# Moving the fixed places of layer norm, transpose and node products of the next four graphs in the first pass of a two-layer graph kernel

## The reference: what is computed

```python
D = jnp.abs(x[:, :, None, :] - x[:, None, :, :])
h = jnp.einsum('bijc,oc->bijo', D, W1) + b1
m = jnp.mean(h, axis=(0, 1, 2))
v = jnp.mean((h - m) ** 2, axis=(0, 1, 2))
h = (h - m) / jnp.sqrt(v + EPS) * g1 + be1
h = _leaky(h)
s = jnp.einsum('bijo,uo->biju', h, W2)[..., 0] + b2[0]
s = jnp.where(A_init > 0, s, NEG)
A = jax.nn.softmax(s, axis=-1)
```

## Time and profile before

| what | value |
|---|---|
| median of three runs | 1147.15 us (1144.66 to 1148.58) |
| the profiled execution: time | 1145.85 us |
| its span in the trace | 1143.7 us |
| PE busy | 1055.3 us, 92% of the span |
| DVE busy | 1037.4 us, 91% |
| ACT busy | 1002.7 us, 88% |
| POOL busy | 558.6 us, 49% |

### The profile page before, as it was taken

One profiled execution on the slowest core, in us unless ns is written; L12 is line 12 of the kernel. 1 busy time (PEld: TensorE's weight loads), 2 busy tenths in 40 slices (PEclk: granted clock), 3 DMA queues, 4 the chain that ended last, 5 costly groups with the idle time before them and its releaser, 6 DMA issues.

```text
span 1143.7 us, 17677 instructions
## 1 busy us (share of the span) xinstructions
PE 1055.3 (92%) x6486; PEld 473.0 (41%) x6486; DVE 1037.4 (91%) x1382; ACT 1002.7 (88%) x1268; POOL 558.6 (49%) x314
## 2 busy tenths in 40 slices
PE   3999999999999999999999989999999999965997
PEld 1333333333333433333333444233333333355997
DVE  5999999999999999999999975999999999845887
ACT  4888999999999999999999969999999999814987
POOL 6586668777767867767777700111122213101420
PEclk9999999999999999999999989999999999987999
DMA  6443444444444444444444497999999999650012
GB/s 180 165 158 156 166 168 173 176 157 183 177 169 185 170 175 157 184 179 173 164 166 194 179 354 247 354 350 318 351 331 335 344 328 347 238 155 1 29 48 74
DMA packets 99059, 233.30 MB, mean 204 GB/s; under 512 B 9120, under 2 KB 46464, under 8 KB 98976
## 3 DMA queue, kind: packets, MB, share of 16 engines
q1 hardware_dynamic: 86704, 219.97, 52.4%
q0 software_dynamic: 2240, 7.34, 1.7%
q10 hardware_dynamic: 10032, 4.89, 1.6%
HBM read 124.43 MB, written 107.74 MB: 203 GB/s over the span
## 4 chain that ended last, share of the span: by engine, by line
PE 50%; DVE 27%; ACT 15%; issue 7%; ACTq 1%; POOL 0%; DMA 0%; DVEq 0%
PE psum L767 17%; DVE store L294 11%; PE psum L777 9%; ACT store L654 7%; PE psum L781 7%; DVE plain_st L1075 5%; PE psum L877 4%; ACT store L573 3%; PE psum L757 1%; PE psum L985 1%; DVE store L1107 1%; PE psum L967 1%; PE psum L950 1%; PE psum L968 1%; DVE ln_st L1012 1%
## 5 line engine op out<-in xcount | busy, mean ns | idle before, releaser
L294 POOL TENSOR_TENSOR store<-h_ext 128x2048 f32<-128x2048 f32 (+1 forms) x96 | 386.7, 4030 | 119.8 <-PE psum L767 115.9
L767 PE MATMUL psum<-store,w1tt_sb 128*64 128x512 f32 x1792 | 421.4, 598 | 19.4 <-ACT store L573 19.1
L294 DVE TENSOR_TENSOR store<-psum,h_ext 128x2048 f32<-128x2048 f32 x160 | 363.7, 2273 | 1.3 <-ACT h_ext L543 1.3
L573 ACT ACTIVATE store<-store 128x2048 f32<-128x2048 f32 x160 | 305.0, 1929 | 11.3 <-DVE store L294 8.1
L654 ACT ACTIVATE store<-store,st 128x1024 f32<-128x1024 f32 x192 | 227.9, 1240 | 0.0
L767 PEld LDWEIGHTS psum<-store,w1tt_sb 128*64 128x64 f32 x1792 | 122.2, 136 | 254.6 <-issue 224.8
L777 PE MATMUL psum<-store,w_twice 128*64 128x512 f32 x768 | 201.1, 601 | 7.0 <-DVE early L1040 3.5
L294 DVE TENSOR_TENSOR store<-h_ext 128x2048 f32<-128x2048 f32 x64 | 146.3, 2286 | 17.2 <-PE psum L767 17.2
L1075 DVE BATCH_NORM_STATS2 plain_st<-store 128x6 f32<-128x512 f32 x256 | 160.4, 676 | 0.0
L781 PE MATMUL psum<-early 128*64 128x512 bf16 x1152 | 158.2, 380 | 0.0
L877 PE MATMUL psum<-store,w_rows 128*32 128x512 f32 x1024 | 135.2, 610 | 8.9 <-ACT store L654 8.9
(11 more groups left out here) (163 smaller groups left out, 1129.3 us busy)
## 6 DMA issues: line engine op xcount, KB each, us to landing
kept_products<-store SPq DMA_DIRECT2D x192, 512.0 KB, 2.7
store<-kept_products SPq DMA_DIRECT2D x192, 512.0 KB, 5.5
early<-score_skew POOLq DMA_DIRECT2D x14, 384.0 KB, 6.7
early<-adj SPq DMA_DIRECT2D x16, 256.0 KB, 3.6
early<-adj_t SPq DMA_DIRECT2D x16, 256.0 KB, 3.6
store<-x ACTq DMA_DIRECT2D x16, 256.0 KB, 5.3
out<-early SPq DMA_DIRECT2D x16, 256.0 KB, 2.3
score_skew<-early POOLq DMA_DIRECT2D x14, 128.0 KB, 6.0
```

Of the source, the lines that this page charges most:

```text
L294: return engine.tensor_tensor(t[:, :, 0:steps, :], nodes.unsqueeze(2).broadcast_to([C, 2, steps, N]), windows(h_ext[:, 2 * c, :], STEP * m ...
L573: nc.scalar.activation(t, t, ACT.Abs).then_inc(abs_ready, 1)
L767: last = nc.tensor.matmul(t[MID * g:MID * g + MID, b, :], w1tt_sb[:, 0:MID], diff[slot][:, g, b * BANK:b * BANK + BANK], start=True, stop= ...
```

## The change

One line of numbers:

```diff
-NORM_AT, TURN_AT, EXT_AT, NODE_AT, HIGH_AT, REST_AT, MID_AT, PLACE_AT, LOW_AT = 3, 4, 5, 6, 7, 10, 10, 12, 16
+NORM_AT, TURN_AT, EXT_AT, NODE_AT, HIGH_AT, REST_AT, MID_AT, PLACE_AT, LOW_AT = 2, 3, 5, 6, 8, 11, 11, 12, 16
```

## The result

The changed kernel takes 1166.69 us (median of four runs, 1166.54 to 1166.96) beside 1146.59 us for the kernel before, a ratio of 1.0175 with a 95% interval of 1.0157 to 1.0194. It is 20 us slower, where about 7 us less were forecast. The forecast of the likeliest case was wrong; the time is that of the rival which got a chance of 0.06, the lock between `low` and POOL's difference (whichever of the two starts second stands until the first is over), priced at 1168 us "at worst".

The account below looks back on a forecast made before the run. PE was taken to bound clean stretches and DVE the full ones. Terms −6.2 (clean quads), −0.9 (ends of DVE-bound stretches) and 0 (start) gave −7.1 us, so 1140.0 us beside 1147.15; own range 1137 to 1143, wider range 1136 to 1147.

Parts of the forecast that it names:

- What bounds the kernel: First pass: PE, DVE and ACT nearly full; PE sets the pace in clean stretches, DVE is full in others.
- the two kinds of stretch: Clean stretches, where shortening PE's waits pays, and stretches where statistics or bias fill DVE and the saving vanishes.
- Places 2 and 3: normalise and turn moved sooner: PE's hole before chunk 5 shrinks, 0.78 us per clean quad, −6.2 us over eight.
- clean quad: A quad in a stretch where PE sets the pace; eight were counted, each with one PE hole of 0.98 us.
- The 0.2 us of hole that I left standing: PE's wait before chunk 5, forecast to remain at about 0.2 us in place of 0.98.
- The late start of chunk 2: On PE, chunk 2 starts 0.07 us late for its absolute value, absorbed by the 0.2 us hole.
- Places 8, 11 and 11: high, rest and middle moved later: ACT's wait in high goes, rest delays DVE by 0.34 us; costed at nothing.
- the rival on the slower side: low slips behind POOL's place 17 difference and is blocked, 3.8 us longer; 1153 to 1168 us, chance 0.06.
- PE runs that much sooner: At 113.50 normalise, 1.54 us, fills ACT's idle time; DVE uses only 0.43 us; the start summed to 0.
- The price: Blocked low: 3.8 us longer, DVE slack hides 1.2; 2.6 us a quad in eight quads, 1168 us at worst.

Follow-up runs that it names:

- The other half: Only high, rest and middle a chunk later (8, 11 and 11), normalise and turn left at 3 and 4, against the kernel before: 1144.94 us, ratio 0.9983.

## Why the prediction was wrong, point by point

- **What bounds the kernel**: right, and the two kinds of stretch were the right distinction. The same distinction was then not applied to the lock.
- **Places 2 and 3.** The mechanism was right, and so was its size. The whole change brings 1.01 us a clean quad where the lock is kept away (39.29 to 38.28 us). The other half brings 0.19 of it by itself (39.29 to 39.10), which leaves 0.82 for this one; 0.78 was forecast. The 0.2 us of hole that I left standing is not listed as a wait, but the pair of chunks 4 and 5 takes 3.78 us in place of 3.60. The late start of chunk 2, forecast at 0.07 us, is some 0.2 (a pair of 3.81 against 3.60 us).
- **Places 8, 11 and 11.** Put at nothing; by themselves they brought 2.3 us, 0.2%. The lead of `low` fell to 0.26 us; "0.4 us are left" overstated it.
- **The step that failed** is the margin in the rival on the slower side: "The change pushes `low` 0.34 later and POOL, which hangs on PE, not: 0.4 us are left". POOL does move. After a late chunk 2 the chain over PE to POOL's difference is 1.7 us shorter (29.28 in place of 30.98 us), and DVE's own, 29.7 us, cannot follow. The 0.77 us was read in clean quads, where DVE waits 1.86 us for PE at the count of chunk 7 and can come sooner by that much when PE does. In quad 3 the lead was 0.77 as well, but the wait that kept it was 0.43: together 1.2 us of room against 1.7. I had the parts: "PE runs that much sooner, of which DVE can use only its 0.43 us wait" stands in the prediction, as a gain in time that is lost, and was not carried over to POOL, which hangs on PE. The first block came there, at 143 us.
- **The second half of the failure** is the view of quads as independent. I asked what one block costs; with the new places a block makes the next. That the entry could be at one place and the price be paid in every later clean quad was not considered, so the chance of 0.06 was far too small.
- **The price.** One block is as priced, 3.65 us longer. That the sum of 1168 us lies near the measured 1166.69 is in part luck. I took 2.6 us for each of eight clean quads and added them to the time of before. Against the unblocked quad of the new places a blocked one costs 2.29 us (40.57 against 38.28), but against the quad of before only 1.28 (39.29). On the other side 11 quads were blocked and not eight, and where DVE has no slack a block costs the whole: from `low` 3 to `low` 4 it was 45.40 us in place of 41.74, and from 8 to 9 45.39 in place of 41.73.
- **The lock.** The Trainium skill, SBUF — State Buffer, section "Who interferes with whom", says that the second to issue is blocked for the whole of the other's instruction. The rows agree: the 4.06 us end 0.28 us behind POOL's 4.20 us that began 0.42 us before, and so do the 3.65 us where POOL began 0.84 us before.

## What to carry to other kernels

Before moving work that makes one engine run ahead, list the pairs of instructions on two other engines that exclude each other, and read their distance in every kind of stretch, the full ones above all, from the last point that both depend on. A margin that a wait maintains is gone when the wait is gone. And where a loop can be in two modes, a small local change is priced by the mode it leaves the loop in, not by its own length: look for one long instruction that repeats once a period.

## What the runs showed of the hardware that I had not expected

- A DVE subtraction of 256 columns with two SBUF operands took 4.06 us in place of 0.40 when POOL's 2048-column subtraction had begun 0.42 us before it; begun 0.26 us after `low`'s own start, POOL's took 4.23 us and `low` 0.41, so neither lost anything measurable. With one of its operands in PSUM the same subtraction took 0.41 us when POOL's had begun 0.41 us before it, and 0.41 us wholly inside one of POOL's.
- The sign of a quarter to half a microsecond decides over 2.3 us a quad (40.57 against 38.28), and one delay of 1.2 us over 13 us of the whole time.
- A pair of chunks on PE whose second operand was ready only as the first product ended took 3.81 or 3.78 us in place of 3.60, although no wait is listed. What inside PE takes the 0.2 us stays open.
